# A vision tower's patch stage with attention's shared keys and norm statistics in it, the last image's Q, K and V within the first chunk, and the class tail split

## The reference

```python
outs = [_level(x, idx, W, b, p, GP) for idx, W, b, p in Ws]
n_tokens = outs[0].shape[1]
outs = [outs[0]] + [_interp_linear(o, n_tokens) for o in outs[1:]]
y = jnp.concatenate(outs, axis=-1)
return y @ Wf.T + bf
...
h = jnp.concatenate([jnp.broadcast_to(cls_tok, (h.shape[0], 1, h.shape[2])), h], axis=1)
h = h + _L0_attn_ref(_layernorm(h, axis=-1), ...)
h = h + _L0_ffn_ref(_layernorm(h, axis=-1), ...)
h = h + _L1_attn_ref(_layernorm(h, axis=-1), ...)
h = h + _L1_ffn_ref(_layernorm(h, axis=-1), ...)
```

```python
xt = jnp.concatenate([x, jnp.broadcast_to(sc_token, (B,) + sc_token.shape[1:])], axis=1)
qkv = (xt @ W_qkv).reshape(B, N1, 3, H, Dh)
attn = jax.nn.softmax(jnp.einsum('bhqd,bhkd->bhqk', q, k) * scale, axis=-1)
out = jnp.einsum('bhqk,bhkd->bhqd', attn, v)
return out[:, :N, :] @ W_proj + b_proj   # reshaped by heads in between
```

## Time and profile before

| | us |
|---|---|
| median of 3 runs | 858.36 |
| lowest and highest | 856.07, 864.34 |
| the profiled execution | 859.04 |
| its span | 857.4 |

### The profile page before, as it was taken

How to read it: one execution, slowest core, us unless ns; L and a number is a source line. 1 busy time by engine, 2 the same in 40 slices (tenths; PEclk the granted TensorE clock), 3 DMA queues, 4 the chain that set the end, 5 groups by cost and what they waited for, 6 DMA issues and landing times. The chain is left out here.

```text
span 857.4 us, 11952 instructions
## 1 busy us (share of the span) xinstructions
PE 743.1 (87%) x4352; PEld 510.2 (60%) x4353; DVE 285.0 (33%) x605; ACT 218.3 (25%) x474; POOL 141.4 (16%) x194
## 2 busy tenths in 40 slices
PE   4509798999999989989999999998969989799970
PEld 4304594555555544438999999863445566377760
DVE  0001423444444248872233233204621243022221
ACT  2200221333343314334444444002410001022210
POOL 6760300011011003330000000000044211301113
PEclk9855699999999989999999999999868997799995
DMA  8700000000000003002988986005765732101102
GB/s 213 175 4 0 1 1 1 1 2 1 1 2 1 1 0 75 1 0 67 256 253 255 258 254 199 1 1 207 180 163 185 279 159 84 60 28 37 32 18 78
DMA packets 27909, 75.77 MB, mean 88 GB/s; under 512 B 7695, under 2 KB 17884, under 8 KB 26688
## 3 DMA queue, kind: packets, MB, share of 16 engines
q1 hardware_dynamic: 24912, 71.41, 28.3%
q0 software_dynamic: 2960, 3.84, 1.7%
HBM read 69.61 MB, written 5.63 MB: 88 GB/s over the span
## 5 line engine op out<-in xcount | busy, mean ns | idle before, releaser
L1243 PE MATMUL banks<-slots,soft_w 96*128 (+1 forms) x768 | 90.9, 275 | 1.6 <-PEq L996 1.6
L1243 PEld LDWEIGHTS banks<-slots,soft_w 96*128 96x128 f32 x768 | 89.8, 192 | 1.8 <-issue 1.8
L1303 DVE COPY eo<-banks 32x192 f32 x128 | 45.3, 354 | 106.6 <-PE banks L1254 103.6
L1289 ACT ACTIVATE hid<-banks,soft_b 128x128 f32<-128x128 f32 x192 | 55.5, 368 | 61.4 <-PE banks L1243 61.3
L759 DVE TENSOR_REDUCE nm<-banks 128x2 f32<-128x906 f32 x48 | 52.9, 1103 | 48.6 <-PE banks L557 48.6
L1254 PE MATMUL banks<-soft_w,hid 128*128 128x192 f32 x384 | 67.5, 326 | 0.0
L725 ACT ACTIVATE pt<-banks 128x1024 f32<-128x1024 f32 (+1 forms) x48 | 49.1, 1023 | 66.1 <-PE banks L583 66.1
L1254 PEld LDWEIGHTS banks<-soft_w,hid 128*128 128x128 f32 x384 | 61.7, 190 | 0.0
L82 PE MATMUL banks<-dense 128*128 128x512 bf16 x165 | 44.1, 419 | 9.5 <-PEq L2151 8.8
L557 PE MATMUL banks<-kt,qt 32*128 32x453 f32 x192 | 49.4, 590 | 3.1 <-DVE nm L759 1.7
L583 PE MATMUL banks<-qa,kt 32*128 32x256 f32 (+1 forms) x384 | 51.8, 386 | 0.0
(11 more groups left out here) (261 smaller groups left out, 1019.5 us busy)
## 6 DMA issues: line engine op xcount, KB each, us to landing
soft_w<-in_sw SPq DMA_DIRECT2D x64, 576.0 KB, 5.5
hy_band<-in_hband SPq DMA_DIRECT2D x6, 1540.0 KB, 7.5
switch_wi<-in_wi SPq DMA_DIRECT2D x1, 4608.0 KB, 25.2
switch_wo<-in_wo SPq DMA_DIRECT2D x1, 4608.0 KB, 16.4
hy_x_spread<-x_rows SPq DMA_DIRECT2D x24, 128.5 KB, 5.2
dwc_spread<-dispatch_cls SPq DMA_DIRECT2D x1, 1536.0 KB, 9.2
sorted_x<-zeros SPq DMA_DIRECT2D x16, 96.0 KB
tile_x<-sorted_x SPq DMA_DIRECT2D x15, 96.0 KB, 1.9
```

Of the source, the lines that this page charges most:

```text
L1243: mm = pe.matmul(ps[:, 2 * (r % 2) + j // 3, (j % 3) * P:(j % 3 + 1) * P], k.w1[r][:, d, j * P:(j + 1) * P], rhs, start=d == 0, stop=d == ...
L1289: ins = act.activation(hid[:, r % 2, j, :], ps[:, 2 * (r % 2) + j // 3, (j % 3) * P:(j % 3 + 1) * P], ACT.Gelu, bias=k.b1[:, ds(i * R + r, ...
L1303: dve.tensor_copy(eo[SL * r:SL * (r + 1), b, ds(i, 1), :].rearrange("p e d -> p (e d)"), ps[SL * b:SL * (b + 1), 4 + r, 0:D]).then_inc(eo_ ...
```

## The change

It touches the patch stage and attention, with a small edit in the norm that hyena and switch share.

- Patch stage: the first half of the level-0 gathers is issued before phi's norm operations. z1 and z2 are one tile z (rows 0 to 63 level 1, row 64 the bias, rows 96 to 111 level 2, the rest zero), and up1 and up2 one matrix up; the eight tiles of h take four interpolation products of 384 columns, issued first with start=True, and the level-0 products add to them. Level 0 goes half by half, the second half by pairs of images on two engines. ScalarE has the copies that VectorE had, and phi's diagonals and factor come after the first half's copy by image. Between the halves stand 8 fillers, the shared keys and values of attention, and 26 fillers (FILL_TOK). VectorE makes the statistics and moments for attention's norm here.
- kt, vt and phi_factor are allocated for both stages. vt's zeros and ones come by DMA (vt0, 2.56 MB) instead of memsets.
- phi's scaling runs on GpSimd in attention.
- Attention: Q, K, V and V2 of images 0 to 2 come first, those of image 3 between the four scores of chunk 0; then the class row. max_rows(0) is ahead of the class row's turn.
- The class tail is inside the last, empty turn of the chunk loop.
- Norm.tensor holds the 16 fillers, in pieces between waits for the statistics.

```diff
@@ Norm.tensor
+        keep_busy(k, pe, bank, 5)
+        if not moments_known:
+            pe.wait_ge(self.stats, 5)
+            keep_busy(k, pe, bank, 3)
+            pe.wait_ge(self.moments, 5)
+            keep_busy(k, pe, bank, 4)
+        pe.wait_ge(self.veps, 1)
+        keep_busy(k, pe, bank, 4)
@@ stage_tok, gpsimd
+                for j in range(G_TOK):
+                    pool.indirect_dma_start(g0[:, 0, j, :], None, a["x0"],
...
                 phi.rnorms(pool)
-                for j in range(32):
+                for j in range(G_TOK):
+                    pool.indirect_dma_start(g0[:, 1, j, :], None, a["x0"],
...
@@ stage_tok, tensor
+                pe.wait_ge(bf_in, 16 * B)
+                phi.spread(pe, 0)
+                for j in range(JT):
+                    for p in range(PAIRS_):
+                        pe.matmul(ps[:, h_bank(j, p), 0:2 * D], up[:, j * P:(j + 1) * P],
+                                  z[:, 2 * p:2 * p + 2, :].rearrange("q b d -> q (b d)"), start=True, stop=False)
+
+                pe.wait_ge(by0, 1)
+                pe.wait_ge(phi.wide_r, 2)
+                turn0(0, range(PAIRS_))
+                pe.wait_ge(xt0a, 1)
+                for p in range(PAIRS_):
+                    embed0(0, p)
+                pe.wait_ge(yr0a, 1)
+                for p in range(PAIRS_):
+                    add0(0, p)
+                pe.wait_ge(k.s_dense, 1)
+                keep_busy(k, pe, 0, 8)
+                pe.wait_ge(k.s_attn_w, 16 * N_ATTN_W)
+                pe.wait_ge(yr0a, 1)
+                shared_keys(k, pe, ksc_m, v3_m)
+                keep_busy(k, pe, 0, FILL_TOK)
+
+                pe.wait_ge(by0, 2)
+                pe.wait_ge(ksc_r, HC)
+                pe.wait_ge(v3_r, 1)
+                turn0(1, range(PAIRS_))
+                pe.wait_ge(xt0a, 2)
+                embed0(1, 0)
+                pe.wait_ge(xt0v, 1)
+                embed0(1, 1)
+                pe.wait_ge(yr0a, 2)
+                add0(1, 0)
+                pe.wait_ge(yr0v, 1)
+                add0(1, 1)
@@ stage_tok, scalar
+                act.wait_ge(got0a, 16 * G_TOK)
+                act.activation(g0b[:, 0, :, :].rearrange("p b (g c) -> p b g c", c=3),
+                               g0[:, 0, :, :].rearrange("p g (b c) -> p b g c", b=B), ACT.Copy).then_inc(by0, 1)
+                phi.diagonals(act)
+                phi.copy_factor(act, 0)
...
+                for p in range(PAIRS_):
+                    copy_h(0, p)
+                act.wait_ge(k.s_attn_w, 16 * N_ATTN_W)
+                copy_shared_keys(k, act, ksc_m, v3_m, ksc_r, v3_r)
+
+                act.wait_ge(got0b, 16 * G_TOK)
...
+FILL_TOK = 26
@@ alloc_attn
-        (k.one_row[:, :], "one_row"), (k.sct[:, :, :], "sct"))]
+        (k.one_row[:, :], "one_row"), (k.sct[:, :, :], "sct"), (k.vt[:, :, :], "vt0"))]
@@ stage_attn, gpsimd
-                pool.memset(vt[:, :, :], 0.0).then_inc(zero, 1)
+                norm.gpsimd(pool)
                 pool.memset(nm[:, :, :, :], 0.0).then_inc(zero, 1)
                 pool.memset(otc[:, :, :], 0.0).then_inc(zero, 1)
-                pool.wait_ge(zero, 3)
-                pool.memset(vt[:, :, DH:HEADS * VW:VW], 1.0).then_inc(ones_r, 1)
-                norm.gpsimd(pool)
+                pool.wait_ge(k_r, 1)
+                scale_phi(k, pool)
@@ stage_attn, tensor
+                scores(0, 0)
+                q_product(LAST, 0, 2)
+                q_product(LAST, 1, 3)
+                scores(0, 1)
+                q_product(LAST, 2, 4)
+                k_product(LAST, 0, 5)
+                scores(0, 2)
+                pe.wait_ge(q_r, HC * LAST + 2)
+                k_product(LAST, 1, 2)
+                k_product(LAST, 2, 3)
+                scores(0, 3)
+                pe.wait_ge(q_r, HC * B)
+                v_product(LAST, 4)
+                pe.wait_ge(k_r, HC * LAST + 1)
+                v2_product(LAST, 5)
...
+                        if i == 1 and n == CHUNKS:
+                            cls_sums()
                         if i == 2 and n >= 1:
                             spread(n - 1)
+                        if i == 3 and n == CHUNKS:
+                            cls_project()
                         if i == 3 and n >= 1 and n % HC == 0:
                             project(n // HC - 1)
@@ layout
+        "up": np.concatenate([upsample(64, 256), np.ones((1, 256), np.float32), np.zeros((31, 256), np.float32),
+                              upsample(16, 256), np.zeros((16, 256), np.float32)]),
```

More of the change, by code:

```diff
@@ L369, in store @@
+                dve.wait_ge(hr, 3)
+                for t in (1, JT + 1):
+                    dve.bn_stats(k.stats[:, t, :], k.h[:, t, :]).then_inc(stats, 1)
+                dve.wait_ge(stats, NT)
+                for t in range(NT):
+                    dve.bn_aggr(k.mv[:, t, :], k.stats[:, t, :]).then_inc(moments, 1)
+FILL_TOK = 26
 def store(k, out):
@@ L500, in _ @@
                                        start=d == 0, stop=d == DC - 1)
[L501 to L514 removed]
+                    mm.then_inc(q_m, 1)
@@ L515, in _, with v2_product @@
+                def v2_product(b, bank):
+                    for d in range(DC):
+                        mm = pe.matmul(ps[0:98, bank, 0:D], k.x2[:, d, b, :], k.wv[:, d, :],
+                                       start=d == 0, stop=d == DC - 1)
+                    mm.then_inc(v2_m, 1)
+                pe.wait_ge(xq_r, NORM_BANKS)
+                pe.wait_ge(x2_r, 1)
+                for b in range(B - 1):
                     for c in range(HC):
@@ L517, in _ @@
                             pe.wait_ge(q_r, (b - 1) * HC + c + 1)
-                        for d in range(DC):
-                            mm = pe.matmul(ps[:, c, 0:L], k.wq[:, d, c * P:(c + 1) * P], xq[:, d, b, :],
-                                           start=d == 0, stop=d == DC - 1)
-                        mm.then_inc(q_m, 1)
+                        q_product(b, c, c)
                     for c in range(HC):
@@ L634, in _ @@
                 mm.then_inc(sc_m, 1)
-                for i in range(4):
-                    scores(0, i)
-                    keep_busy(k, pe, 2, 3)
+                pe.wait_ge(v2_r, LAST)
+                max_rows(0)
+                pe.wait_ge(v_r, B)
+                pe.wait_ge(v2_r, B)
+                keep_busy(k, pe, 2, 3)
                 pe.wait_ge(pcr_r, 1)
```

406 lines of the change are left out of this document (209 added, 197 removed).

## The result

| | us |
|---|---|
| before, median of 4 runs | 859.73 (856.07 to 864.34) |
| changed, median of 4 runs | 825.29 (824.30 to 827.22) |
| ratio, with its 95% interval | 0.9599 (0.9547 to 0.9652) |
| the profiled execution, its span | 827.22, 825.6 |

What follows compares the result with a forecast made beforehand. Time lay where TensorE waits for level-0 gathers or runs at half clock. Savings of 21.2, 6.3, 3.6 and 0.8 us sum to 31.9; from the 858.36 median that gives 826.5 us, range 818 to 837.

Steps and rivals of the forecast that it cites:

- Gathers of half one: Patch stage: the first half's level-0 gathers land at 42.5 us, 1.0 of it for vt0's rows; bounds 37.7 and 47.5.
- rival 2: Patch stage: half one's gathers land late, at 47.5; +5 us, so 831.5; chance 0.12.
- The chain behind it: Patch stage: TensorE's work after half one's landing, phi's spread included, runs from 42.5 to 68.5, later than the gathers (59.9).
- Half two to the first Q product: Patch stage's end and attention's start: from 68.5 to the first Q product at 84.5, before 105.74; 21.2 us saved.
- The charge for the memsets: Attention's norm: memsets of nm and otc beside xn cost 0.8 us, bounds 0 and 1.0.
- The last image: Attention: last image's products inside chunk 0; first Q product to chunk loop 37.0 us, before 43.26; 6.3 saved.
- Rival 5: Attention's prologue: scores wait for copies of the last image, six gaps of 1 us; +6, so 832.5; chance 0.04.
- The tail: Behind attention's chunk loop: class product stands before project, whose add is the end; 3.6 us saved (3.0 to 4.5).
- Clock at the soft experts' start: Soft experts: less idle time before the first logits, which ran at clock 0.52; 0.8 us saved (bounds -1 and 2).
- Rival 1: Patch stage: granted clock stays 0.50 to the end of the fillers; 10 us more, so 836.5; chance 0.17.
- Rival 3: Patch stage: TensorE's chain is short enough that half two's gathers still bound; -8 us, so 818.5; chance 0.12.
- Rival 4: Attention: Q, K, V and first scores stay at 1.2 GHz; no gain or slower, 860 and more; chance 0.03.

Runs made afterwards that it cites:

- g4: Changed kernel with GpSimd's two operations of phi's norm ahead of all 32 level-0 gathers again, as before the change; 828.40 us.
- g1: Changed kernel with phi's diagonals and factor copies on ScalarE ahead of the wait for half one's gathers; 820.94 us.
- g3: Changed kernel with vt by memset, loads reordered, phi's spread between the halves, nm and otc memsets later, 36 fillers; 822.25 us.
- e1: Changed kernel with the class tail put back behind the chunk loop, with its nine fillers; 849.71 us, against 847.99 for the changed kernel beside it.
- series one: First four follow-up kernels, on one chip: the changed kernel repeated and three variants of it; the repeat took 847.99 us.

## Why the prediction was right, and where its steps were off

**Gathers of half one: right.** 42.5 forecast; the last packet ended at 42.45 and 41.57, ScalarE's copy began at 43.37 and 42.84. The price of vt0 (4.8 in the sum) came out at 3.8 (memset) and 4.7 (loads late). The formula behind it is less good than its number: issue plus a time failed when the issue was moved by 4.26 us (g4). The Trainium skill (DMA: Bandwidth & Descriptors, "Queues, rings and completion order") has an engine take turns between queues at the granularity of packets. The direction of the price agrees with what the prediction drew from that. A longer delay, rival 2, did not come: even with vt0 twice half one was there at 44.17.

**The chain behind it: right.** Forecast and measured: end of the spread 49.3, 50.3; of the up products 52.4, 53.1; start of the keys 59.5 (62.2 less their 2.7), 61.07; the second half's transposes 68.5, 69.35. At the keys, 1.6 us late, 0.9 came with the landing; the eight dense products ahead of them took 3.58 for 1.7, since the clock was at half from 57.7 to 61.1, and half one with its adds was quicker than forecast (4.6 us for 5.4). The sum had 0.7 for half clock. Among the signs stands a first transpose "near 50", which the prediction's own sum (52.4) contradicts; 53.06 and 51.98 bear out the sum. g1 shows the largest term: diagonals, spread and factor, on the path by the order on ScalarE alone, are worth 4.4 us or more.

**Half two to the first Q product: right in sum, one charge in the wrong place.** The second half's transposes began 0.8 late, attention's veps at 76.93 against about 76.5, and the first Q product at 84.10 against 84.5. The terms of the first part add up to 8.6, not 8.3, so the sum should have had 8.3 and not 8.0 there; 7.6 were measured. From veps on it was 7.2 for 7.9. xn took 3.23 us for 2.69: 0.54 for the memsets, charged at 0.8. In this row the first of the nine is the long one (0.92 us against 0.37), so it waited about as long as nm's memset takes (0.52) and not for otc's 0.41 too. The Trainium skill (SBUF — State Buffer, "SBUF: two separate sides") has the loser of the shared ports wait for the whole instruction. For the first memset the trace agrees; the second, which the prediction added to make 0.95, cost xn nothing. But in g3, with xn back at 2.70, the transposes were still 3.8 us behind veps, as in the changed kernel: they wait for the nine dense products at half clock (4.00 us), not for xn. The charge for the memsets had no place on the path; the 1.0 for half clock was the real one.

**The last image: right mechanism, one term mis-sized.** 37.92 us for 37.0. The three images took 21.65 (forecast 21.45), and from the first score to the loop 16.27 (forecast 15.55). From one score to the next it is 2.89 us: 0.96 of score and 1.93 of two products, which at the pace of the first images take 1.73 (six products 5.2), so each switch costs 0.2, 0.6 in all. V and V2 took 2.15 us for 2.0, and the dense products with the wait for the exp of the class row 0.95 for 0.8. Rival 5, gaps of 1 us each, did not come: no score waits for a copy.

**The tail: right in mechanism, the clock under-read.** 4.43 us for 3.6. I let project run at 1.95 to 3.5 us and took the middle; it ran at full clock, 2.11. The 3.46 us that the prediction has for project before leave out its last record; with it the timeline has 3.90. Project right behind the wait for ot ran at half clock in both profiles (3.90 before, 4.21 in e1), behind the class product at full clock in eleven of twelve, so the order matters, though it doesn't fix the clock.

**Clock at the soft experts' start: right at the start, but the 0.8 us of the sum did not come.** The first logits ran at 0.43 us in place of 0.85 and 0.7 us sooner after the stage's start, but the stage as a whole was 0.4 longer.

**Rival 1 (half clock through the fillers) fell**: 1.00 from 62 on. **Rival 3** would need more than a short chain: in g1, 4.4 us ahead, half two's gathers are still no bound. **Rival 4** fell at the window 122 to 270.5.

**What the range didn't hold.** In series one the changed kernel took 838.81 and 840.08 us in two executions and 855.9 and 861.43 in the other two, 2.4% below before at best rather than 4%. ScalarE's standstill of 22 us puts the first Q product 12.5 us later (96.59 for 84.10), which is about the first two; what made the other two longer still is open. No row of the kernel before hints at it, and the prediction had no such case. It costs 12.5 us now because levels 2 and 1, half one, the keys and half two all pass through ScalarE, each behind the one before; before the change level 0 was VectorE's and waited until 61.95 for its gathers anyway. That the kernel before had the same standstill in that series and hid it is possible, but was not seen: its runs there have no trace.

## What to carry to other kernels

When a stage is broken up so that work starts earlier, list what still stands in order on the copying engine: here three lines moved ahead of a wait on ScalarE gave as much as taking 2.56 MB from under the gathers. Dense fillers are worth what the products behind them lose at half clock, and nothing more; measure both. Work moved from one place on the path to another, as the shared keys were, can cost in the new place what it saves in the old (2.7 us for 2.6): look at what takes its place.

## What the runs showed of the hardware

- ScalarE stood still from 11.3 to between 40.47 and 40.56 us in all four profiles of one series, with TensorE's result there at 18.4, and in none of the nine profiles of changed kernels in the others. What holds it stays open. It ended 1.3 to 2.1 us before the last packet of vt0 started (41.9 to 42.6), but loads that ended at 37.6, 42.8 and 49.9 us in another series, on another chip, brought none.
- With 10.4 MB in SP's queue, the last gather of half one was 7.3 to 8.1 us old when its copy began, with the loads late 2.5. Where it was issued 4.26 us later under the same load, it was copied only 1.4 us later. In eight profiles its last packet ended within 0.2 us of the load's last packet of 19,968 bytes.
- The granted clock fell to 0.53 in a tail whose instructions ran at full pace in eleven other profiles, and 1.6 us went with it.
- The granted clock of a window can read 1.00 while products go at half pace. In the changed kernel the four records of the spread at 46.58 took 3.70 us, in g3 the same four 1.88. The trace of the changed kernel has no record of the clock before 50.9 us, so the 1.00 of a window ahead of that says nothing. The first line is the window around the spread in the changed kernel, the second the row of g3:

```profile
44.00:50.00 6.00, 3.42 (x4) 1.30 (x5) 0.00 (x0) 2.43 (x8) 4.48 (x5) 1.00 0.09 8
```

```profile
49.24 1.88 PE L1067 MATMUL banks<-phi_diag,ones 128*96 128x512 f32 x4
```
